# Attention over 32 tiles on one core: the last three half-transposes move from the DMA queue to PE

## The reference, cut to what matters

```
x: (4, 128, 32, 32) float32;  per batch: C = 128 channels, N = 1024 positions
h    = group_norm(x, 32 groups) * gamma + beta
q, k, v = rows of (w_qkv @ h + b_qkv)
attn = softmax(q.T @ k / sqrt(128))          # 1024 x 1024 per batch
out  = w_proj @ (attn @ v.T).T + b_proj
return x + out
```

## Time and profile before

| | us |
|---|---|
| median of 3 runs | 132.26 (130.9, 132.26, 132.26) |
| the profiled execution | 131.82 |
| its span in the trace | 129.8 |
| PE busy | 114.6 (88%) |
| DVE busy | 93.9 (72%) |
| ACT busy | 87.9 (68%) |
| POOL busy | 85.4 (66%) |
| DMA transposes | 64, median 3.4 from issue to landing |

### The profile page before, as it was taken

The page is one execution under the profiler, slowest core; times in us unless marked ns, Lnnn a source line. Parts: engine busy times, 40 slices in busy tenths (PEclk is TensorE's granted clock), DMA queues, the critical chain, the costliest instruction groups (busy, mean ns, idle before and its releaser), DMA issues.

```text
span 129.8 us, 3100 instructions
## 1 busy us (share of the span) xinstructions
PE 114.6 (88%) x1161; PEld 80.6 (62%) x1161; DVE 93.9 (72%) x242; ACT 87.9 (68%) x121; POOL 85.4 (66%) x60
## 2 busy tenths in 40 slices
PE   0599887988998999999989999999899999987671
PEld 0373544556775677667646776776467767767550
DVE  3659799999856967998569579776695797774222
ACT  1304429999778787877986878879868788785000
POOL 6010004879999897999759888998657666788200
PEclk9999999999999999999999999999999999999999
DMA  3692000797999999999999999999999999999990
GB/s 94 170 346 119 0 3 17 146 123 147 192 153 187 184 197 129 240 191 192 149 224 194 187 192 200 179 146 234 190 169 132 243 192 114 197 232 155 179 246 20
DMA packets 70670, 21.43 MB, mean 165 GB/s; under 512 B 68352, under 2 KB 69120, under 8 KB 70656
## 3 DMA queue, kind: packets, MB, share of 16 engines
q1 hardware_dynamic: 69888, 20.98, 89.9%
q10 hardware_dynamic: 704, 0.26, 0.8%
q0 software_dynamic: 64, 0.00, 0.0%
HBM read 2.36 MB, written 2.10 MB: 34 GB/s over the span
## 4 chain that ended last, share of the span: by engine, by line
PE 49%; DVE 23%; DMA 9%; ACT 7%; SPq 6%; issue 2%; ACTq 0%
DVE row_max L432 10%; PE scores L617 7%; DMA ptT<-p_hl 6%; PE o_ps L637 6%; PE scores L619 6%; PE scores L618 6%; PE o_ps L633 5%; PE o_ps L632 5%; SPq L232 4%; DVE t_lo L421 4%; DMA wqkv_sb<-in_L_conv_w_qkv_dram 3%; PE o_ps L643 3%; ACT probs L343 3%; DVE out_sb L453 3%; ACT p_hl L350 2%
## 5 line engine op out<-in xcount | busy, mean ns | idle before, releaser
L285 POOL TENSOR_TENSOR p_hl<-probs,p_hl 128x1024 f16<-128x1024 f32 x32 | 68.1, 2130 | 27.0 <-ACT p_hl L350 26.7
L432 DVE TENSOR_REDUCE row_max<-scores 128x1 f32<-128x1024 f32 x32 | 39.1, 1222 | 19.3 <-PE scores L619 19.1
L343 ACT ACTIVATE probs<-scores,exp_bias,esc 128x1024 f32<-128x1024 f32 x32 | 38.5, 1202 | 19.2 <-DVE exp_bias L435 19.2
L350 ACT ACTIVATE p_hl<-probs 128x1024 f16<-128x1024 f32 x32 | 33.8, 1057 | 1.0
L632 PE MATMUL o_ps<-v_hi,ptT 128*128 128x128 f16 x256 | 32.0, 219 | 0.4 <-DVE v_lo L427 0.4
L633 PE MATMUL o_ps<-v_lo,ptT 128*128 128x128 f16 x256 | 32.0, 219 | 0.0
L617 PE MATMUL scores<-z_hi,t_hi 128*128 128x512 f16 x64 | 24.3, 379 | 2.8 <-DVE t_lo L421 1.7
L632 PEld LDWEIGHTS o_ps<-v_hi,ptT 128*128 128x128 f16 x256 | 25.0, 98 | 2.3 <-issue 0.8
L633 PEld LDWEIGHTS o_ps<-v_lo,ptT 128*128 128x128 f16 x256 | 25.0, 98 | 0.2
L619 PE MATMUL scores<-z_hi,t_lo 128*128 128x512 f16 x64 | 24.3, 379 | 0.0
L618 PE MATMUL scores<-z_lo,t_hi 128*128 128x512 f16 x64 | 24.3, 379 | 0.0
(11 more groups left out here) (109 smaller groups left out, 134.0 us busy)
## 6 DMA issues: line engine op xcount, KB each, us to landing
out_dram<-out_sb SPq DMA_DIRECT2D x7, 256.0 KB, 2.6
x_sb<-in_x_dram SPq DMA_DIRECT2D x3, 512.0 KB, 4.8
ptT<-p_hl SPq DMA_TRANSPOSE x64, 3.4
x_sb<-in_x_dram SPq DMA_DIRECT2D x2, 256.0 KB, 3.3
out_dram<-out_sb SPq DMA_DIRECT2D x1, 192.0 KB, 2.0
wqkv_sb<-in_L_conv_w_qkv_dram ACTq DMA_DIRECT2D x1, 128.0 KB, 4.0
wqkv_sb<-in_L_conv_w_qkv_dram ACTq DMA_DIRECT2D x1, 64.0 KB, 3.5
wp_sb<-in_L_conv_w_proj_dram ACTq DMA_DIRECT2D x1, 64.0 KB, 3.8
```

What stands on the lines that cost most here:

```text
L285: nc.gpsimd.tensor_tensor(p_hl[:, g % RING, 1], probs[:, g % RING], p_hl[:, g % RING, 0], ALU.subtract).then_inc(plo_ready, 1)
L343: nc.scalar.activation(probs[:, g % RING], scores[:, g % SLOTS], ACT.Exp, bias=exp_bias[:, g:g + 1], scale=esc[:], accum_out=row_sum[:, g: ...
L350: nc.scalar.activation(p_hl[:, g % RING, 0], probs[:, g % RING], ACT.Copy).then_inc(phi_ready, 1)
L432: nc.vector.tensor_reduce(row_max[:, g:g + 1], scores[:, g % SLOTS], AX_X, ALU.max).then_inc(max_ready, 1)
```

## The change

The DMA transposes hi(30), hi(31) and lo(31) are no longer issued. PE transposes these three halves against a float16 identity (`ident16`, one DVE copy at the start), 8 transposes of 128x128 each, into `scores` slots that are free by then; the result is copied to `ptT` by DVE (hi(30), lo(31), read as 512 uint32) or ACT (hi(31), 1024 float16). The low half of tile 31 is made by DVE in place of POOL. In the tail each product with V now stands ahead of the turn of the tile before it. The main loops up to g = 31 are the same.

```
 SP    for g in range(G):
           wait(sp, pv_ready, g - PT_RING + 1)
+          if g < LAST - 1:                      # LAST = 31
               ... hi(g) ...
+          if g < LAST:
               ... lo(g) ...
 POOL  for g in range(G):
-          p_low(g)
+          if g < LAST:
+              p_low(g)
 ACT   (after its loop)
+          act.wait_ge(hi_turned, 2)
+          act.wait_ge(pv_ready, LAST - PT_RING + 1)
+          act.wait_ge(hi_moved, 1)
+          nc.scalar.activation(ptT[:, LAST % PT_RING, 0]..., turned_half(LAST, 0), ACT.Copy
+                               ).then_inc(hi_moved, 1)
 DVE   at the start:
+          nc.vector.tensor_copy(ident16[:], ident32[:]).then_inc(ident16_ready, 1)
       after its loop, which now ends at g = 31:
+          scale_output(LAST - 4)
+          dve.wait_ge(hi_turned, 1)
+          dve.wait_ge(pv_ready, LAST - PT_RING)
+          nc.vector.tensor_copy(ptT[:, (LAST - 1) % PT_RING, 0]...bitcast(U32),
+                                turned_half(LAST - 1, 0).bitcast(U32)).then_inc(hi_moved, 1)
+          add_input(LAST - 4)
+          inverse_sum(LAST)
+          scale_output(LAST - 3)
+          dve.wait_ge(phi_ready, LAST + 1)
+          dve.wait_ge(lo_transposed[LAST % RING], 16 * (LAST // RING))
+          dve.wait_ge(plo_ready, LAST)
+          nc.vector.tensor_tensor(p_hl[:, LAST % RING, 1], probs[:, LAST % RING],
+                                  p_hl[:, LAST % RING, 0], ALU.subtract).then_inc(plo_ready, 1)
+          scale_output(LAST - 2)
+          add_input(LAST - 3)
+          dve.wait_ge(lo_turned, 1)
+          nc.vector.tensor_copy(ptT[:, LAST % PT_RING, 1]...bitcast(U32),
+                                turned_half(LAST, 1).bitcast(U32)).then_inc(lo_moved, 1)
+          add_input(LAST - 2)
+          scale_output(LAST - 1)
+          scale_output(LAST)
+          add_input(LAST - 1)
+          add_input(LAST)
 PE    in values(g):
-          pe.wait_ge(hi_transposed[g % RING], 16 * (g // RING + 1))
+          if g < LAST - 1:
+              pe.wait_ge(hi_transposed[g % RING], 16 * (g // RING + 1))
+          else:
+              pe.wait_ge(hi_moved, g - LAST + 2)
       ... and lo_moved in place of lo_transposed for g = LAST ...
+      def turn_high(g):
+          pe.wait_ge(phi_ready, g + 1)
+          for k in range(TILES):
+              last = nc.tensor.transpose(turned_half(g, 0)[:, k * P:(k + 1) * P],
+                                         p_hl[:, g % RING, 0, k * P:(k + 1) * P], ident16[:])
+          last.then_inc(hi_turned, 1)
       after its loop, which now ends at g = 31:
+          turn_high(LAST - 1)
+          values(LAST - 3)
+          turn(LAST - 4)
+          values(LAST - 2)
+          turn(LAST - 3)
+          turn_high(LAST)
+          pe.wait_ge(plo_ready, LAST + 1)
+          ... 8 transposes of the low half of LAST ...
+          last.then_inc(lo_turned, 1)
+          turn(LAST - 2)
+          values(LAST - 1)
+          values(LAST)
+          turn(LAST - 1)
+          turn(LAST)
```

More of the change, by code:

```diff
@@ L10 @@
 F16 = mybir.dt.float16
+U32 = mybir.dt.uint32
 AX_X = mybir.AxisListType.X
@@ L25 @@
 LAG = 4
+LAST = G - 1
 Z_BOUND = math.sqrt(GROUP * N)
@@ L116, in attention_block @@
         ptT = sb("ptT", [P, PT_RING, 2, TILES, P], F16)
+        ident16 = sb("ident16", [P, P], F16)
         oT_sb = sb("oT_sb", [P, 2, P])
@@ L192, in attention_block @@
         lo_transposed = [sem(f"lo_transposed{i}") for i in range(RING)]
+        hi_turned = sem("hi_turned")
+        lo_turned = sem("lo_turned")
+        hi_moved = sem("hi_moved")
+        lo_moved = sem("lo_moved")
+        ident16_ready = sem("ident16_ready")
         pv_ready = sem("pv_ready")
@@ L202, in stat, with turned_half @@
             return o_ps[:, 0, 2 * P + which:2 * P + which + 1] if b < 2 else misc[:, which, 0:1]
+        def turned_half(g, which):
+            return scores[:, g % SLOTS, which * HALF:(which + 1) * HALF].bitcast(F16)
         def wait(eng, s, value):
@@ L230, in _ @@
                 wait(sp, pv_ready, g - PT_RING + 1)
[L231 to L236, removed]
+                if g < LAST - 1:
+                    sp.wait_ge(phi_ready, g + 1)
+                    sp.dma_start(ptT[:, g % PT_RING, 0], p_hl[:, g % RING, 0], transpose=True
+                                 ).then_inc(hi_transposed[g % RING], 16)
+                if g < LAST:
+                    sp.wait_ge(plo_ready, g + 1)
+                    sp.dma_start(ptT[:, g % PT_RING, 1], p_hl[:, g % RING, 1], transpose=True
+                                 ).then_inc(lo_transposed[g % RING], 16)
                 done = g - LAG - CT
@@ L374, in _ @@
                     t_high(b + 1, s - 6)
+            act.wait_ge(hi_turned, 2)
+            act.wait_ge(pv_ready, LAST - PT_RING + 1)
+            act.wait_ge(hi_moved, 1)
+            nc.scalar.activation(ptT[:, LAST % PT_RING, 0].rearrange("p k q -> p (k q)"), turned_half(LAST, 0), ACT.Copy
+                                 ).then_inc(hi_moved, 1)
         @block.vector
@@ L542, in _ @@
             nc.vector.tensor_tensor(bo[:], bp_c[:], o_ps[:, 0, 0:1], ALU.add).then_inc(w_ready, 1)
-            for g in range(G + LAG + 1):
+            for g in range(G):
                 b, s = divmod(g, TILES)
@@ L563, in _ @@
                     group_var(1)
-                if s in (2, 3) and b < B:
+                if s in (2, 3):
                     v_low(b, s - 2)
@@ L633, in values @@
                     nc.tensor.matmul(dst, hi, v_lo[:, keys], start=False, stop=False)
-                pe.wait_ge(lo_transposed[g % RING], 16 * (g // RING + 1))
+                if g < LAST:
+                    pe.wait_ge(lo_transposed[g % RING], 16 * (g // RING + 1))
+                else:
+                    pe.wait_ge(lo_moved, 1)
                 for k in range(TILES):
@@ L681, in _ @@
             nc.tensor.matmul(o_ps[:, 0, 0:1], wpT[:], bv_c[:], start=False, stop=True).then_inc(bo_psum, 1)
-            for g in range(G + LAG + 1):
+            for g in range(G):
                 b, s = divmod(g, TILES)
[L685 to L688, removed]
+                if g == 1:
+                    pe.wait_ge(wmat_ready, 1)
+                score_tile(g)
                 if g > LAG:
                     turn(g - LAG - 1)
-                if LAG <= g < G + LAG:
+                if g >= LAG:
                     if g == LAG:
@@ L694, in _ @@
                     values(g - LAG)
[L695 to L723, removed]
@@ new lines, in _ @@
+                if s in (1, 2):
+                    if g < TILES:
+                        pe.wait_ge(w_ready, 2)
+                    pe.wait_ge(tlo_ready, b * 2 + s)
+                    v_products(b, s - 1)
+                if g in (2, 3):
+                    if g == 2:
+                        group_mean(1)
+                    else:
+                        group_var(1)
+                    for _ in range(KEEP_WARM):
+                        nc.tensor.matmul(o_ps[:, 1, 0:HALF], ones16[:], warm[:], start=True, stop=True)
@@ new lines, in _ @@
+                if s == 5 and b + 2 < B:
+                    pe.wait_ge(vlo_ready, b * 2 + 1)
+                    group_mean(b + 2)
+                if s == 6 and b + 2 < B:
+                    pe.wait_ge(vlo_ready, b * 2 + 2)
+                    group_var(b + 2)
+                if s == 6 and b + 1 < B:
+                    pe.wait_ge(mean_ready, min(b + 3, B))
+                    pe.wait_ge(vlo_ready, b * 2 + 1)
+                    t_products(b + 1, 0)
+                if s == 7 and b + 1 < B:
+                    pe.wait_ge(vareps_ready, min(b + 3, B))
+                    pe.wait_ge(vlo_ready, b * 2 + 2)
+                    t_products(b + 1, 1)
@@ new lines, in _ @@
+            pe.wait_ge(ident16_ready, 1)
+            turn_high(LAST - 1)
[5 more added lines that the diff above has]
+            pe.wait_ge(plo_ready, LAST + 1)
+            for k in range(TILES):
+                last = nc.tensor.transpose(turned_half(LAST, 1)[:, k * P:(k + 1) * P],
+                                           p_hl[:, LAST % RING, 1, k * P:(k + 1) * P], ident16[:])
+            last.then_inc(lo_turned, 1)
```

11 lines of the change are left out of this document (7 added, 4 removed).

## The result

The changed kernel takes **130.12 us** (median of 4 runs, 129.52 to 130.25) against 131.83 (median of 4, 130.90 to 132.26) for the kernel before on the same chip: a ratio of **0.989, 95% interval 0.985 to 0.994**. The profiled execution took 130.25 with a span of 128.5; it is the slowest of the four, whose spans go from 127.7 to 128.5. The forecast was 130.6 with a span of 128.45, so both numbers fit. The way there did not: PE never waits for lo(29), it waits for lo(30). That is rival D, to which the prediction gave 0.08.

The account below looks back on a forecast made before the run. The end stood on transfers lo(29) and lo(31); the change removes the second. Landing of lo(29) at 120.6 + 7.85 = 128.45, 1.35 us under 129.8; from 131.82 that says 130.5, named 130.6, range 129.4 to 131.9.

Parts of the forecast that it names:

- rival D: Tail: the stall falls on lo(30), landing at 123.3, values(30) 1.1 us late; end 128.6, time 130.6; chance 0.08.
- The fixed rest behind the last wait: Tail after lo(29) lands: 3.86 us to the start of the last low part, then 3.82 to the end.
- L: Landing of lo(29), which values(29) waits for: 121.05 before, forecast between 120.2 and 121.05, taken as 120.6.
- L + 7.85: End of the kernel counted from the landing of lo(29), with the last store 0.15 us late.
- rival A: Tail: no stall ahead of lo(29), PE never waits; end 127.5, time 129.5; chance 0.13.
- The transposes: PE's float16 transposes in the tail: one every 0.056 us, 8 in 0.45 us, all 24 in 1.34.
- Rival C: PE's 24 transposes don't pipeline: at 0.33 us each, 4.3 us slower than before, 136.1; chance 0.05.
- The copies: PSUM copies: DVE 0.67 us, ACT 1.06, DVE's low half of tile 31 1.22; slack 0.2 on DVE, 0.6 on ACT.
- rival B: Tail: copies use up their slack, lo(29) still lands at 121.05; gain 0 to 0.9 us, 130.9 to 131.8; chance 0.18.
- The order: Tail: values(28) gains about 0.5 us; add(27) ends at 118.7, not 117.78, so values(29) starts at 118.76.
- No wait of its own: hi(30) and hi(31) had none on the chain; removing them only brings DMA time for lo(30), issued 118.3, not 118.99.
- the prediction's count: Nine instruction-queue packets for 2,322 PE instructions, one per 258; 16 more bring the stall 0.5 to 1.5 us earlier, with values(28)'s earlier start.

Follow-up runs that it names:

- control: The changed kernel itself, unedited, run a second time beside other runs; 129.94 us, ratio 0.987 against the kernel before.
- order-only kernel: Kernel before with only the new tail order on PE and DVE, all half-transposes still by DMA, low halves by POOL; 132.22 us, ratio 1.002.

## Why the prediction was right in time and wrong in its wait

- **The fixed rest behind the last wait, right.** In the working the end lies 7.85 - 2.52 = 5.33 behind the start of the low part of values(30); measured 128.5 - 123.19 = 5.31. Where lo(29) is the last wait (the kernel with lo(30) on PE), the end is 7.73 behind that low part's start, forecast 7.80. But L + 7.85 as a whole does not hold for the change: with L at 119.50 it gives 127.35, or 127.5 from the 119.66 at which PE is there, 1.0 less than measured. The wait for lo(30) is missing in it. That its L + 2.52 = 123.12 lies beside the measured 123.19 is luck.
- **L itself, failed.** "The stall comes some 0.5 to 1.5 us earlier. It then falls into hi(29) or the middle of lo(29)." It came 1.3 us later, after lo(29) had landed: PE takes it up at 119.79, and had no wait. L fell from 121.05 to 119.50, by 1.55 us and not by 0.45, and lies outside the stated 120.2 to 121.05; it is the 119.5 that the prediction gives for lo(29) without a stall. That would have been rival A, 127.5; the start of lo(30)'s low part at 122.25 in place of 123.19 gives 128.5 - 0.94 = 127.56.
- **Where the rest went.** The stall fell on lo(30): issued at 118.40, 4.75 us, landing at 123.15. The prediction had the issue (118.3) and the slowest landing (123.3), but took 3.4 us for it, since it needed the stall for lo(29). That is D, with its L of 119.5 and its end of 128.6, measured 128.5. The forecast's 128.45 was near by chance: it has a stall on lo(29) where one on lo(30) came. Nor is the cost of a stall a constant that would have saved it: 0.9 us in this trace and 0.5 in the control for lo(30), 1.36 in the trace where it hit lo(29).
- **The transposes, right.** Eight take 0.61 us with the last one's own 0.22, thus 0.056 from start to start, the lower bound. Rival C is out: 24 at 0.33 would show a span near 134. The Trainium skill, TensorE: Matmul & The Clock Gate, Part 4: PE-mode transpose, gives 275 ns each inside a kernel; these rows show 0.22 us of own duration and a new start every 0.056, and the latter is what PE pays. The same section says that transposes do not count for the clock gate. In this trace the granted clock is 1.00 during the 16 transposes and behind them (the windows view: length, busy us of PE, its weight loads, DVE, ACT and POOL, granted clock, DMA share, GB/s):

```profile
120.30:121.40 1.10, 1.10 (x21) 1.08 (x20) 0.67 (x3) 0.40 (x1) 0.00 (x0) 1.00 2.49 101
...
123.00:126.00 3.00, 2.41 (x34) 2.03 (x34) 1.08 (x3) 0.00 (x0) 0.00 (x0) 1.00 0.04 13
```

  So that rule costs this kernel nothing, with matmuls right before and right behind the 16; only the last of the page's 40 slices is lower (0.8), when PE has stopped. The 1.2 GHz that the prediction gives for the start rests on the pace of the earlier trace rows alone: for 10.0 to 13.9 us of the kernel before, the windows view has a granted clock of 1.00.
- **The copies, right.** 0.68 and 0.69 (forecast 0.67), ACT 1.02 (1.06), DVE's low half 1.22 (1.22). Their slack held, so rival B is out.
- **The order, half seen.** Its price, add(27) at 118.7, was met (118.44 + 0.35) and paid: hi(29) had landed at 118.56, and values(29) started at 118.90, forecast 118.76. That the order earns nothing while lo(31) is a transfer, and half of the whole once it is not, the prediction did not say.
- **hi(30), right in its cost, wrong in its use.** "No wait of its own": back on the queue it costs nothing measurable. But the prediction had lo(30) issued earlier because hi(30) is not ahead of it; with hi(30) ahead it is issued at 118.36 all the same.

What stays open is why the stall came later. 84 more PE instructions moved it forward by 4.8 us in the changed kernel and by 3.3 in the one before (by the prediction's count, 84 / 258 of the 11.3 us that the expectation takes between two packets are 3.7, an estimate), so its tie to PE's program is shown. The tie is loose, though, and the prediction took it as tight. Asked in narrow windows, the DMA view gives the start of each packet of the instruction queue, and the windows view what PE had begun by then. In the kernel before the nine packets are 9.4 to 13.4 us apart. In all fourteen traces the one of the tail comes when PE has begun 1,085 to 1,125 matmuls: 1,085 before (at 119.05 us) and 1,102 with the 84 instructions, 1,125 in the change (at 120.70), 1,119 in the control and 1,103 with the 84. The packet ahead of it agrees (107.54 us and 961 matmuls before, 107.67 and 962 in the change), so all of the difference arises with the last one.

By the prediction's count, 16 more instructions ahead of values(28) should have moved it some 0.7 us forward. The order-only kernel, with no PE instruction more than before, has it at 119.40 and 1,105 matmuls, between the two, so part of the shift may come with the order; one trace does not show it. The changed program differs in other ways too (its code is longer and placed otherwise, on several engines), and no run separated these. The stall makes 0.4 of the 0.9 us between the two traces of the changed kernel (spans 128.5 and 127.6); the rest is there before the first score matmul.

## What to carry to other kernels

Before a transfer is taken away from the end of a chain, look at what makes the slow ones slow: here transfers that took 4.3 to 5.0 us where the others took 3.4 were hit by something that has a place in time, and that found the next one. Price a tail as "last landing + the fixed rest", and work the rest out for each transfer that could be the last, not only for today's. When the profile puts a wait down to a transfer, look when that transfer landed: at 118.90 it was an add. And try the parts alone: here two of five pieces (hi(30), the low half on DVE) bring nothing that can be told, and reordering pays only after the transfers that hid it are gone.

## What the runs showed of the hardware

- DMA transposes stop almost completely, 0 to 17 GB/s for 1.0 to 1.5 us, beside a single packet of the instruction queue of 0.02 MB. The page counts 9 such packets a span, 10 in the changed kernels with 84 or more instructions added. The transfer that is hit lands 4.3 to 5.0 us after its issue in place of 3.4. Splitting 14 matmuls into 56, far from the tail and without more columns, moves the stall by 3.3 us in the kernel before (one trace of each) and by 3.9 to 4.8 in the changed one (two of each).
- A float16 128x128 transpose on PE starts every 0.056 us, like a matmul of that shape; 16 take 0.9 us, and 16 more, done twice, 0.9 more. The granted clock is 1.00 through them.
- A DVE copy of 128x1024 float16 from PSUM, read as 512 uint32, takes 0.68 us; ACT's copy of the same 1024 elements 1.02.
